# An expert pipeline on one Trainium2 core: every handoff one round apart, eight result buffers, scatters tied to the next round

## The reference

```python
logits = x @ gate_weight.T
probs = softmax(logits)                         # 1024 tokens here, 64 experts
routing_weights, selected_experts = lax.top_k(probs, 8)
routing_weights = routing_weights / routing_weights.sum(axis=-1, keepdims=True)
for each expert e:                              # 96 inner channels, 256 outer
    gate, up = split(x @ gate_up_weights[e], 2)
    out = (silu(gate) * up) @ down_weights[e]
    final = final + combine[:, e] * out
```

## Time and profile before

| | |
|---|---|
| timed runs, median (range) | 522.57 us (521.33 to 523.16) |
| profiled execution, span on the page | 576.6 us |
| PE busy | 477.4 us, 83% of the span |
| DVE, ACT, POOL busy | 342.7, 305.9, 212.3 us |
| first steady round's rows on DVE, last round's rows on DVE | 366.5 and 524.7 us |

### The profile page before, as it was taken

The page is one execution under the profiler, slowest core; times in us unless marked ns, Lnnn a source line. Parts: engine busy times, 40 slices in busy tenths (PEclk is TensorE's granted clock), DMA queues, the critical chain, the costliest instruction groups (busy, mean ns, idle before and its releaser), DMA issues. The chain is left out here.

```text
span 576.6 us, 10371 instructions
## 1 busy us (share of the span) xinstructions
PE 477.4 (83%) x3073; PEld 351.1 (61%) x3073; DVE 342.7 (59%) x1204; ACT 305.9 (53%) x854; POOL 212.3 (37%) x224
## 2 busy tenths in 40 slices
PE   4586999999899899999983766987988888888666
PEld 1366767877787678788653423765665666655322
DVE  4768496596685894795793564544355454553033
ACT  3456787885966887779864201333244343444200
POOL 0344110041114631025584642245444455445600
PEclk9799999999999999999996788999899899899879
DMA  8920862000301102002998739884444444330097
GB/s 283 411 70 19 167 131 74 1 1 0 76 1 54 69 30 73 2 1 74 345 404 291 278 107 298 227 288 129 111 115 115 113 128 127 107 95 13 19 363 304
DMA packets 47318, 79.49 MB, mean 138 GB/s; under 512 B 8266, under 2 KB 31127, under 8 KB 46880
## 3 DMA queue, kind: packets, MB, share of 16 engines
q1 hardware_dynamic: 36864, 55.34, 31.1%
q0 software_dynamic: 7680, 16.93, 8.2%
q10 hardware_dynamic: 2720, 6.55, 3.5%
HBM read 56.54 MB, written 26.44 MB: 144 GB/s over the span
## 5 line engine op out<-in xcount | busy, mean ns | idle before, releaser
L620 POOL DMA_INDIRECT pair_rows<-eout,dest x93 | 91.8, 987 | 99.5 <-ACT eout L634 78.2
L833 ACT ACTIVATE sact<-ps 128x192 f32<-128x192 f32 (+1 forms) x50 | 16.3, 325 | 122.7 <-remote 73.6
L1323 DVE SCALAR_TENSOR_TENSOR aact<-sact,wcol,ps 128x96 f32<-128x96 f32 x96 | 26.0, 311 | 92.6 <-issue 87.1
L1685 PE MATMUL ps<-wts,xg 128*64 (+1 forms) x512 | 71.5, 342 | 3.7 <-DVE copy_gu L1346 2.2
L691 ACT ACTIVATE lg<-lg,mneg 128x128 f32<-128x128 f32 (+1 forms) x128 | 56.4, 443 | 26.1 <-DVE mneg L1029 21.5
L1685 PEld LDWEIGHTS ps<-wts,xg 128*64 128x64 f32 x512 | 53.0, 143 | 16.5 <-issue 9.5
L541 POOL DMA_INDIRECT slot_rows<-rows,pair_slot x48 | 47.9, 998 | 37.2 <-issue 24.1
L1512 PE MATMUL ps<-oT,wo_sb 128*128 128x256 f32 x240 | 54.4, 380 | 0.0
L1706 PE MATMUL ps<-wts,aT 96*64 96x256 f32 (+1 forms) x256 | 49.8, 395 | 4.4 <-issue 3.4
L1512 PEld LDWEIGHTS ps<-oT,wo_sb 128*128 128x128 f32 x240 | 44.6, 190 | 6.2 <-ACT oT L634 0.7
L634 ACT ACTIVATE lg<-lg,rinv 128x128 f32<-128x128 f32 (+1 forms) x128 | 45.9, 448 | 2.5 <-issue 1.7
(11 more groups left out here) (237 smaller groups left out, 1184.4 us busy)
## 6 DMA issues: line engine op xcount, KB each, us to landing
wts<-in_experts_dram SPq DMA_DIRECT2D x22, 640.0 KB, 8.0
xrow<-slot_rows SPq DMA_DIRECT2D x192, 65.0 KB
pairs<-pair_rows SPq DMA_DIRECT2D x16, 512.0 KB, 11.2
wts<-in_experts_dram ACTq DMA_DIRECT2D x10, 640.0 KB, 6.1
slot_rows<-zero SPq DMA_DIRECT2D x1, 4160.0 KB, 24.2
wT<-in_wq_t_dram SPq DMA_DIRECT2D x4, 512.0 KB, 6.5
wq_raw<-in_wq_l_dram SPq DMA_DIRECT2D x1, 2048.0 KB, 14.6
wo_sb<-in_wo_l_dram SPq DMA_DIRECT2D x1, 2048.0 KB, 20.5
```

Of the source, the lines that this page charges most:

```text
L620: nc.gpsimd.indirect_dma_start(out=pair_d, out_offset=bass.IndirectOffsetOnAxis(ap=dest[:, d:d + 1], axis=0), in_=out_rows(d), in_offset=N ...
L1685: ins = nc.tensor.matmul(ps[h * R:(h + 1) * R, 2 + u % 2, k * I2:(k + 1) * I2], xg[u % len(xg)][:, k, cc, h * R:(h + 1) * R], moving, star ...
```

## The change

- Eight result buffers in place of six, as four pairs; two silu buffers in place of one.
- The product of gate and up goes to three PSUM banks in turn in place of two (gu_bank); the turned results share one bank.
- PE's iteration g is turn_rows(g), turn_act(g-2), gate_up(g-1), down(g-3), and the loop has one iteration more. ACT's is silu(g-1), copy_turned(g-2), copy_down(g-2), copy_out(g-3).
- On DVE find_rows of both groups moves behind both weighs, and copy_gate_up of a group goes ahead of a weigh.
- POOL waits, ahead of the first group of a round r from 4 to 23, until the down products of the whole round r+1 are done.

```diff
-    NOUT = 6
+    NOUT = 8
+        PLAIN = 8
+        def gu_bank(u):
+            return 2 + u % 2 if u < PLAIN else (5, 2, 3)[(u - PLAIN) % 3]
+        def gu_before(u):
+            return u - 2 if u < PLAIN else u - 3
+        PACED = range(TOPK // 2, NR - 3)
...
             for d in range(NDBL):
+                r = round_of[group_of[d]]
+                if r in PACED and group_of[d] == ROUNDS[r][0]:
+                    pool.wait_ge(dn_done, ROUNDS[r + 1][-1] + 1)
                 pool.wait_ge(out_copied, group_of[d] + 1)
...
             def silu(u):
-                if u >= 1:
-                    act.wait_ge(act_ready, u)
+                if u >= 2:
+                    act.wait_ge(act_ready, u - 1)
...
-            for g in range(NR + 2):
+            for g in range(NR + 3):
                 us = ROUNDS[g - 1] if 1 <= g <= NR else []
-                outs = ROUNDS[g - 2] if g >= 2 else []
-                for a in outs:
-                    copy_turned(a)
+                outs = ROUNDS[g - 2] if 2 <= g < NR + 2 else []
                 for u in us:
                     silu(u)
                 for a in outs:
+                    copy_turned(a)
+                for a in outs:
+                    copy_down(a)
+                for a in ROUNDS[g - 3] if g >= 3 else []:
                     copy_out(a)
-                for u in us:
-                    copy_down(u)
...
             for g in range(NR + 1):
                 ins_ = ROUNDS[g] if g < NR else []
-                for x in ins_:
-                    copy_turned_rows(x)
-                    find_rows(x)
                 us = ROUNDS[g - 1] if g else []
                 for k in range(max(len(us), len(ins_))):
+                    if k < len(ins_):
+                        copy_turned_rows(ins_[k])
+                        copy_gate_up(ins_[k])
                     if k < len(us):
                         weigh(us[k])
-                    if k < len(ins_):
-                        copy_gate_up(ins_[k])
+                for x in ins_:
+                    find_rows(x)
...
-            for g in range(NR + 2):
+            for g in range(NR + 3):
...
-                for a in outs:
+                for a in ROUNDS[g - 3] if g >= 3 else []:
                     down(a)
```

More of the change, by code:

```diff
@@ L214, in adaln_attn_ffn @@
         o = 16 * KIB
-        xg = [at(f"xg{i}", [P, 2, CC, P], off) for i, off in enumerate((take(2 * KIB), take(2 * KIB), r3 + 10 * KIB, rows_off[0] + NOUT * KIB))]
+        xg = [at(f"xg{i}", [P, 2, CC, P], off) for i, off in enumerate((take(2 * KIB), take(2 * KIB), r3 + 10 * KIB, rows_off[0] + (NOUT - 2) * KIB))]
         wcol = at("wcol", [P, (NE + MORE) // 2], take(384))
-        sact = at("sact", [P, 2, I], take(2 * I * 4))
+        sact = [at(f"sact{i}", [P, 2, I], off) for i, off in enumerate((take(2 * I * 4), row_off + 2 * KIB))]
         aact0 = take(2 * I * 4)
@@ L233, in adaln_attn_ffn @@
         assert o <= spare + 5 * KIB
-        eout = at("eout", [P, NOUT, C], rows_off[0])
+        eout_pair = [at(f"eout{i}", [P, 2, C], off) for i, off in enumerate([rows_off[0] + 2 * i * KIB for i in range(NOUT // 2 - 1)] + [row_off])]
         eout_first = at("eout_first", [P, 3, C], r3 + 12 * KIB)
@@ L358, in adaln_attn_ffn @@
         NR = len(ROUNDS)
+        round_of = {g: r for r, gs in enumerate(ROUNDS) for g in gs}
         TABLE_AT = 5
@@ L371, in out_rows @@
         def out_rows(d):
-            return eout_first[:, d] if d < 3 else eout[:, d % NOUT]
+            return eout_first[:, d] if d < 3 else eout_pair[d % NOUT // 2][:, d % 2]
+        PLAIN = 8
[4 more added lines that the diff above has]
+        PACED = range(TOPK // 2, NR - 3)
         block = ctx.enter_context(nc.Block())
@@ L822, in copy_turned @@
                 n = len(GROUPS[a])
-                act.wait_ge(at_done, a + 1)
+                act.wait_ge(at_done, ROUNDS[round_of[a]][-1] + 1)
                 if a >= 2:
                     act.wait_ge(dn_done, a - 1)
-                copy(aT[a % 2][0:I, 0:n, :], ps[0:I, 4 + a % 2, 0:n * P].rearrange("p (k t) -> p k t", k=n)).then_inc(at_copied, 1)
+                copy(aT[a % 2][0:I, 0:n, :], ps[0:I, 4, a % 2 * 2 * P:(a % 2 * 2 + n) * P].rearrange("p (k t) -> p k t", k=n)).then_inc(at_copied, 1)
             def silu(u):
@@ L845, in copy_out @@
                 else:
-                    copy(eout[:, d % NOUT:d % NOUT + n, :], ps[:, 6 + a % 2, 0:n * C].rearrange("p (k c) -> p k c", k=n)
+                    copy(eout_pair[d % NOUT // 2][:], ps[:, 6 + a % 2, 0:n * C].rearrange("p (k c) -> p k c", k=n)
                          ).then_inc(out_copied, 1)
@@ L1644, in turn_act @@
                 pe.wait_ge(act_ready, a + 1)
-                if a >= 2:
-                    pe.wait_ge(at_copied, a - 1)
-                if a == TABLE_AT:
-                    pe.wait_ge(cols_read, 2)
+                if a == ROUNDS[round_of[a]][0] and a:
+                    pe.wait_ge(at_copied, a)
                 for k in range(len(GROUPS[a])):
-                    ins = T_(ps[0:I, 4 + a % 2, k * P:(k + 1) * P], aact[a % 2][:, k, :])
+                    ins = T_(ps[0:I, 4, (a % 2 * 2 + k) * P:(a % 2 * 2 + k + 1) * P], aact[a % 2][:, k, :])
                 ins.then_inc(at_done, 1)
@@ L1727, in _ @@
                     pe.wait_ge(cols_ready, 1)
-                    pe.wait_ge(at_copied, g - 1)
                     for k in range(3):
```

23 lines of the change are left out of this document (13 added, 10 removed).

## The result

| | before | after |
|---|---|---|
| timed runs, median (range) | 521.95 us (520.45 to 523.16) | 538.85 us (537.55 to 540.99) |
| ratio, 95% interval | | 1.028 (1.024 to 1.033) |
| profiled execution: its own time, span | see below | 538.46 us, 536.7 us |

The change made the kernel slower by 16.9 us. Forecast was 532.0 with a range of 507 to 537: the sign was right, and so was the place of the largest part, the end of the expert stage. The size fell 6.9 us short, and the time lies 1.9 us above the range.

The account below looks back on a forecast made before the run. The prediction took PE to bound the steady rounds, at 6.14 us a round at full clock. 522.57 us plus 10.3 for the pace wait's tail, less 1 for small waits, all else 0, gave 532, range 507 to 537.

Parts of the forecast that it names:

- late signals: PE's signals 2.7 and 3.2 us late in steady rounds while POOL scatters, 1.53 us a round; taken as absent from timed runs.
- Rival A: Late signals are in the timed runs too, so earlier scatters make it faster: 506 to 518 us, taken 512; chance 0.29.
- The floor of a round, 6.14: PE's steady round: 5.84 us of issue plus 0.30 for a register load of 0.59 once in two rounds.
- PE's order, down one iteration later, 0: On PE, without late signals the wait that the later down removes is not there: nothing gained, 0.
- DVE's order 0: Copies of weights ahead of the second weigh on DVE cost 0, hidden by 1.2 us.
- find_rows 0: Later find_rows on DVE frees row buffers later: 0 in steady rounds, at most 1 us in each of five rounds.
- The pace wait, 10.3: POOL's wait leaves sixteen scatters at the end in place of eight: 8 x 1.29 = 10.3 us more tail.
- The signs named: Sixteen end scatters at 1.29 us from round 24's down signal, PE idle 10 us longer, paced scatters within 0.3 us of down.
- Rival C: Row loads come late in the rounds with weights' loads, +5 us on the forecast: 537; chance 0.08.
- Small gains of the steady rounds, -1: Small waits saved in the 23 steady rounds, between -2 and 0 us, taken as -1.
- Rival B: No change: one iteration more of room removes 20 x 0.45 = 9 us of handoff jitter; 521 to 526 us, chance 0.13.

Follow-up runs that it names:

- down_back: The changed kernel without the pace wait, with find_rows early, down and copy_out back in iteration g-2 and ACT's old order; 523.92 us, ratio 0.997.
- no_pace: The changed kernel without the pace wait on POOL, all else as changed; 536.80 us, ratio 1.024.
- again_before: The kernel before, unchanged, profiled a second time; 521.49 us, span 519.7 us.
- copy_out_first: The changed kernel without the pace wait, with find_rows early and, on ACT, copy_out ahead of copy_down; 532.07 us, ratio 1.021.
- no_pace_find_early: The changed kernel without the pace wait and with find_rows right behind each copy of turned rows, as before; 534.00 us, ratio 1.022.
- again_after: The changed kernel, unchanged, timed and profiled a second time; 538.76 us, ratio 1.027.
- down_back_half_rounds: down_back with its last three rounds cut into six of one group; 521.44 us, ratio 0.996 to the kernel before.

## Why the prediction was right, and where it was not

- **That the late signals are not in the timed runs: right**, and the 54.0 us between span and timed runs were the sound reason for it. Rival A, which needed them, fell: no profile after the first has them. All 54 us belong to the one execution.
- **The floor of a round, 6.14 at full clock: right in kind, 0.2 high.** Before runs at 5.94 in most rounds, with no alternate round longer by 0.59, so the register load does not add as it was made to.
- **PE's order, down one iteration later, 0: wrong.** For the steady rounds the argument held (there was no wait to remove; buffers and order in down_back come to -0.3%, within their uncertainty). But the prediction asked only what the move does in a steady round, and gave its price at the end to another edit. An iteration more of pipeline is one iteration more to empty: with copy_out, 7.5 us of the tail.
- **DVE's order 0: not separated.** Down_back keeps the copies of weights ahead of the weigh and loses nothing that can be measured. **find_rows 0: wrong.** Alone it costs 6.3 us of time, 0.22 a round in rounds 10 to 26, and not only in five early rounds. "It keeps up with less to spare" was a count of SP's issues; the buffer's way round (read, freed, issued, landed) was not added up. Inside the changed kernel its undoing gave 1.1 us by the ratios and 2.8 by the medians, neither clear of the noise.
- **The pace wait, 10.3: the size of the tail right (10.4), but charged to one edit where two share it.** The count held. At down in PE's iteration 27, POOL has rounds 25 and 26 left before (eight scatters, from 482.13) and rounds 23 to 26 after (sixteen, from 488.85). The step that failed is the one from this count to the sum: "the difference is 8 x 1.29" stands as the price of the wait, and the later down as 0. Of the eight scatters more, four are there because iteration 27 now does down of round 24, and they stay when the wait is taken out (no_pace); the other four are the wait's. Reckoned from the last load of gate/up weights:

| kernel | scatters left | the first of them behind that load | tail |
|---|---|---|---|
| again_before | 8 | 2.87 | 2.87 + 7 x 1.29 = 11.9 |
| no_pace | 12 | 5.18 | 5.18 + 11 x 1.29 = 19.4 |
| after | 16 | 3.00 | 3.00 + 15 x 1.29 = 22.3 |

  The later down and copy_out cost 7.5: four scatters, and 2.3 us by which the first of them stands later behind gate/up, 1.2 of it for copy_down ahead of the copy (copy_out_first); the other 1.1 were not taken apart. The wait costs 3.0: four scatters, less the 2.2 us by which the burst starts sooner, at down's signal and not behind the copy. So the tail of the whole change was foreseen by a sound count, and what each edit alone would do was not.
- **The signs named**: sixteen at 1.29, the first released by the down signal, came out, but don't show whose price they are. The first scatters of the paced rounds do wait for PE, but start 0.78 to 1.08 us behind the end of the last down matmul (1.38 once), not within 0.3. Rival C's sign, row turns that wait for DMA in rounds 6 to 10, is no stronger after than before (3.0 and 2.8 us); the new waits came later. PE idle for 10 us longer did not come out. PE's timeline ahead of the final sum, again_before and after:

```profile
482.44 1.95 PE L1706 MATMUL ps<-wts,aT 96*64 96x256 f32 x16 [0.39 <-ACT aT L634]
484.31 1.98 PE L1738 MATMUL ps<-x2tm,ident 128*128 128x512 f32 x4
495.66 7.95 PE L1738 MATMUL ps<-pairs,ident 128*128 128x512 f32 x12 [9.36 <-DMA pairs<-pair_rows]
```

```profile
494.58 3.68 PE L1720 MATMUL ps<-wts,aT 96*64 96x256 f32 x16 [1.11 <-ACT eout L648]
498.20 3.56 PE L1752 MATMUL ps<-x2tm,ident 128*128 128x512 f32 x4
513.07 10.18 PE L1752 MATMUL ps<-pairs,ident 128*128 128x512 f32 x16 [11.31 <-DMA pairs<-pair_rows]
```

  PE waits only 2 us longer (11.31 against 9.36), because its own last iteration comes later and ran at the lower of its two clocks, 1.2 GHz: the granted clock is 0.50 from 494 to 498 us, and 1.00 in again_before from 482.4 to 484.4, and the same sixteen down matmuls take 3.68 in place of 1.95 us. The forecast gave PE under 6 us for what is left behind the last gate/up's iteration; from the turn at 488.70 to the end of down it was 9.6. POOL had eight scatters still to do by then (508.19 back in steps of 1.29 to 499.16), so this cost nothing.
- **Small gains of the steady rounds, -1: wrong sign.** Rounds 10 to 26 took 3.4 us more. Taken apart by the profiles, 1.5 of it goes with the pace wait (99.6 against 98.1 in no_pace), 0.7 with the late find_rows (97.4 in no_pace_find_early), and 1.2 stays with an unknown part of the new orders; each step is one profile. Outside the tail the stage took +3.1 in all, 4.1 us off the -1. +9.3 was forecast and +16.9 came; the 3.5 that are left in the profiles are the start, ahead of every edit, which looks like chance (below). A second profile of after has 1.7 less of it and a stage longer by 1.6, and on its chip the medians are 13.5 us apart, which is what after's stage gained.
- **Rival B** fell, since the rounds gave nothing back. **Rival C** was the one that bore on the size, at 0.08: its mechanism is there, priced in too few rounds. That its 537 is the nearest of the four times to 538.85 is partly luck: late rows cost nothing like 5 us inside the changed kernel, and the pace wait's price in the rounds and the start make up the rest.

## What to carry to other kernels

Set the profile's span against the timed runs before reading any wait in it: where they differ by 10%, take no stall and no count of queued work from it without asking whether the timed runs have it. Making a pipeline one stage deeper may cost little in a steady round, but its emptying at the end grows by a round of the queue that ends last (7.5 us here, for rounds of 6); price each edit at the loop's end by itself, by asking what is left when that edit stands alone. When an operation frees a buffer, add up the buffer's whole way round, not only the issue rate of the queue that fills it.

## What the runs showed of the hardware

- In one profiled execution of fourteen, PE's signals came 2.7 and 3.2 us late while GpSimd issued indirect scatters, and the span was 576.6 us in place of 519.7. What brought it on stayed open.
- The start of the expert stage lay between 318.7 and 325.3 us in the thirteen clean profiles, though all do the same work up to there. Down_back and down_back_half_rounds, which are the same kernel up to the last rounds, lie 5.8 us apart. It goes with the clock granted early on: six profiles have a clock of 0.83 in the stretch from 20 to 30 us and begin the stage at 318.7 to 321.6 (again_after is one of them), seven have 0.59 to 0.68 and begin at 322.3 to 325.3. The stretch (columns as in the earlier trace rows) of again_before, after and down_back, which began the stage at 319.1, 322.6 and 325.3:

```profile
20.00:30.00 10.00, 6.82 (x29) 5.46 (x29) 6.64 (x14) 7.54 (x14) 4.86 (x3) 0.83 0.93 365
```

```profile
20.00:30.00 10.00, 5.20 (x19) 4.55 (x20) 6.86 (x11) 4.49 (x7) 3.19 (x2) 0.68 0.97 379
```

```profile
20.00:30.00 10.00, 4.84 (x16) 4.24 (x17) 6.86 (x11) 4.31 (x6) 3.06 (x2) 0.59 0.96 376
```

  PE ran 29 to 31 matmuls in that stretch at the higher figure and 15 to 26 at the lower ones, so the records don't tell which led. It makes a single profile's span uncertain by some 3 us, and is why the table has the stage by itself.
- The scatters of 128 rows never came closer than 1.29 us to each other in any burst (0.98 and 0.30 between), whatever held them.
